# A fused two-attention kernel: maxima 56 units ahead instead of 64, shifts in a group's fourth step, and another end for the last group

## The reference

```python
xn = _layernorm(x)
# A: 8 heads; queries and keys of 128 + 32 dims, both from latents of 32 dims
c_q, c_kv = xn @ W_DQ + b_DQ, xn @ W_DKV + b_DKV
attn = softmax(einsum(q, k) / sqrt(160));  A = (attn @ v_c) @ W_O + b_O
# B: 16 heads of 16 dims. Each token is 'pos' or not, from its query's cosine
# with a guide vector, scaled by the minimum and maximum over all tokens
x_pos, x_neg = masked_attn(pos), masked_attn(~pos)
tok_out = where(pos, x_pos, x_neg)    # each token sees the keys of its own kind
reg_out = (x_pos[:, :5] + x_neg[:, :5]) * 0.5     # the first five tokens
B = concat([reg_out, tok_out]) @ W_proj + b_proj
out = x + A + B
```

## Time and profile before

| | |
|---|---|
| median of three runs | 2928.48 us (2927.09 to 2930.65) |
| the profiled execution | 2925.61 us |
| its span, first to last instruction | 2923.8 us |
| PE busy | 2791.4 us, 95% |
| DVE busy | 2260.7 us, 77% |
| ACT busy | 1649.1 us, 56% |
| POOL busy | 1376.4 us, 47% |
| mean granted TensorE clock | 0.985 |
| chain that ended last | PE 66%, DVE 12%, POOL 12%, issue 4%, DMA 3% |
| PE waits with an empty pipeline | 28.6 us for POOL in the first pass, 15.2 us for shifts, 13.4 us for POOL at the end |

### The profile page before, as it was taken

One profiled execution on the slowest core, in us unless ns is written; L12 is line 12 of the kernel. 1 busy time (PEld: TensorE's weight loads), 2 busy tenths in 40 slices (PEclk: granted clock), 3 DMA queues, 4 the chain that ended last, 5 costly groups with the idle time before them and its releaser, 6 DMA issues.

```text
span 2923.8 us, 45386 instructions
## 1 busy us (share of the span) xinstructions
PE 2791.4 (95%) x16873; PEld 1255.4 (43%) x16873; DVE 2260.7 (77%) x4151; ACT 1649.1 (56%) x1899; POOL 1376.4 (47%) x643
## 2 busy tenths in 40 slices
PE   6888999999999999999999999999999999999997
PEld 4643434443345343453334433453434533344333
DVE  5776887777877888778877788778887788777891
ACT  2444566555655556555665557555665556655674
POOL 6657422692228712395225922278122962259201
PEclk9999999999999999999999999999999999999998
DMA  5524234401352124511344013530244112540001
GB/s 173 188 44 91 70 96 100 87 17 46 101 108 59 33 60 107 114 27 36 88 106 87 18 37 105 103 68 21 64 116 105 36 36 80 115 87 17 22 14 38
DMA packets 129149, 213.45 MB, mean 73 GB/s; under 512 B 47889, under 2 KB 76561, under 8 KB 128753
## 3 DMA queue, kind: packets, MB, share of 16 engines
q1 hardware_dynamic: 125120, 203.21, 29.2%
q10 hardware_dynamic: 3808, 7.34, 0.7%
HBM read 138.31 MB, written 72.50 MB: 72 GB/s over the span
## 4 chain that ended last, share of the span: by engine, by line
PE 66%; DVE 12%; POOL 12%; issue 4%; DMA 3%; ACT 2%; SPq 1%; POOLq 0%; ACTq 0%; DVEq 0%
PE O L1252 20%; PE M L1139 12%; DVE mx L1472 9%; PE M L1133 8%; POOL PTx L848 7%; PE S L1240 6%; PE S L1237 6%; PE M L1167 4%; POOL PT L848 3%; PE M L1217 2%; PE M L1219 2%; PE M L1179 1%; PE M L1185 1%; ACT PT L1002 1%; PE M L1163 1%
## 5 line engine op out<-in xcount | busy, mean ns | idle before, releaser
L1472 DVE TENSOR_REDUCE mx<-M 128x1 f32<-128x512 f32 x3072 | 1949.8, 682 | 374.3 <-PE M L1133 186.0
L1002 ACT ACTIVATE PT<-S 128x1024 f32<-128x1024 f32 x1280 | 1240.1, 1022 | 757.5 <-PE S L1240 480.5
L1139 PE MATMUL M<-KB,QB 50*128 50x512 f32 x2048 | 619.7, 477 | 29.8 <-DVE mx L1472 12.4
L1252 PE MATMUL O<-PT,VB 128*32 128x512 f32 x4096 | 552.3, 611 | 2.3 <-ACT PT L1002 2.3
L1139 PEld LDWEIGHTS M<-KB,QB 50*128 50x128 f32 x2048 | 253.6, 184 | 641.9 <-DVE mx L1472 330.9
L1133 PE MATMUL M<-KA,QA 98*128 98x512 f32 x1024 | 418.6, 458 | 8.0 <-DVE mx L1472 6.5
L1240 PE MATMUL S<-QB,KB 52*128 52x512 f32 x2048 | 377.7, 432 | 8.8 <-ACT PT L1002 7.8
L1002 ACT ACTIVATE PTx<-S 128x1024 f32<-128x1024 f32 x256 | 248.3, 1022 | 194.3 <-PE S L1237 160.7
L1237 PE MATMUL S<-QA,KA 114*128 114x512 f32 x1024 | 318.3, 412 | 15.2 <-DMA QA<-sh_d 15.2
L848 POOL TENSOR_TENSOR PT<-PT,PTx 128x2048 f32<-128x2048 f32 x64 | 293.0, 4578 | 21.3 <-POOL PT L848 10.4
L848 POOL TENSOR_TENSOR PTx<-PTx,PT 128x2048 f32<-128x2048 f32 x64 | 292.1, 4569 | 15.8 <-POOL PTx L848 13.8
(11 more groups left out here) (155 smaller groups left out, 2074.6 us busy)
## 6 DMA issues: line engine op xcount, KB each, us to landing
qk_d<-stg SPq DMA_DIRECT2D x32, 1024.0 KB
KA<-kt_d SPq DMA_DIRECT2D x48, 512.0 KB, 7.3
QB<-qk_d SPq DMA_DIRECT2D x192, 128.0 KB
KB<-qk_d SPq DMA_DIRECT2D x192, 128.0 KB
kt_d<-stg SPq DMA_DIRECT2D x16, 1024.0 KB
RB<-recb_d SPq DMA_DIRECT2D x64, 256.0 KB
PT<-in_x SPq DMA_DIRECT2D x8, 1024.0 KB, 7.1
RB<-rec_d SPq DMA_DIRECT2D x32, 256.0 KB
```

What stands on the lines that cost most here:

```text
L1002: nc.scalar.activation(probs(kind, of_a)[:, 2 * pair:2 * pair + 2, :], Sg[pair][:, :].rearrange("p (j s) -> p j s", j=2), ACT.Exp, scale=S ...
L1139: done = mm(m[:, :], QB[rows, 2 * q + a, at:at + P], KB[rows, 2 * q + a, keys], start=True, stop=True)
L1252: last = mm(O[32 * jj:32 * jj + 32, :], lhs, probs(kind, k)[:, jj, :], start=(c == 0), stop=(c == NC - 1), skip_group_check=True)
L1472: v.tensor_reduce(mx[:, g % 2, unit, kh:kh + 1], m[:, :], AX.X, ALU.max).then_inc(free, 1)
```

## The change

- `prep_jobs`: the 32 first units stand at 13 places, three and two in turn, and the first shift stands two places before the end of the first pass instead of at its end.
- `place` takes the units from one stream over all groups, `LEAD` = 56 units ahead of their step instead of 64. The four steps of batch 0's A that held six units hold four (`FIRST_MAXIMA`); the last batch has units in its steps 48 and 49 of B, which had none.
- `TURN` = 3: every shift stands in the fourth step of a group, not the second. In the first A the last one stands at step 27 instead of 25.
- The last `dn` of a batch stands in B's fifth step instead of the third.
- SP loads the residual of the second half right after it has stored the first half, in B's last group and ahead of `recs` of group 6. POOL adds the constant to it at the end of B, ahead of `clear_z`. `scale` of group 6 comes ahead of the first quad's additions.
- In the first A, the wait for the transfers of constant rows into KB stands ahead of the last shift and not ahead of the first `load_b`.
- The last group of the last batch is finished in another way: PE computes the output blocks from the other groups into the score banks, DVE takes numerators and denominators of the last group from PSUM, 128 queries at a time, inverts and multiplies, PE adds the last product and DVE adds the residual; SP stores block by block. In every batch DVE's inverse of B's group 6 stands after step 60 of B instead of after step 63.

```diff
-    for i in range(16):
-        out[15 + i] += ma[2 * i:2 * i + 2]
-    out[31] += [("fa", "a", 0)]
+    for i in range(13):
+        out[15 + i] += ma[(5 * i + 1) // 2:(5 * i + 6) // 2]
+    out[29] += [("fa", "a", 0)]
...
+LEAD, TURN = 56, 3
...
-FIRST_MAXIMA = (7,) * 4 + (5,) * 12 + (4,) * 2 + (6, 4, 4, 6, 4, 4, 6, 4, 4, 4, 6, 4, 4, 4)
+FIRST_MAXIMA = (7,) * 4 + (5,) * 12 + (4,) * 2 + (4,) * 14
...
-            s[g * NC + 1][2].append(("fa", "b", g + 1))
+            s[g * NC + TURN][2].append(("fa", "b", g + 1))
...
-    s[2][2].insert(0, ("dn", QUADS - 1))
+    for k in range(STEPS_B):
+        place(s[k], "b", LEAD + 4 * (STEPS_A + k), more)
+    s[4][2].insert(0, ("dn", QUADS - 1))
...
 # SP, a_steps
-                if before and g == 0:
-                    load_residual(b, 1)
...
 # SP, b_steps
                 if g == 7:
                     store_out(b, 0, [b_spot(b, last, ("po", c)) for c in range(4)])
-                    if last:
-                        load_residual(b, 1)
+                    load_residual(b, 1)
                 if g:
                     recs(b, "b", g - 1)
...
 # POOL
             if before:
                 clear_z(n)
+            if before:
+                scale(b, "b", GB - 2)
             for i in range(QUADS):
                 add(n, i)
-                if before and i == 0:
-                    residual(b, 1)
-                if before and i < 2:
-                    scale(b, "b", GB - 2 + i)
+                if before and i == 1:
+                    scale(b, "b", GB - 1)
...
 # POOL, end of b_steps
+            residual(b, 1)
...
 # PE
+        def tail():
+            pe.wait_ge(o_done, B * GROUPS - 2)
+            for c in range(4, NC):
+                at = c * P
+                for q in range(QA_):
+                    mm(tail_bank(c), OA[:, q, at:at + P], NA[:, q, :], start=(q == 0), stop=False)
+                mm(tail_bank(c), OB[:, 0, at:at + P], Wp[:, 0, :], start=False, stop=False)
+            pe.wait_ge(o_done, B * GROUPS - 1)
+            for c in range(4, NC):
+                mm(tail_bank(c), OB[:, 1, c * P:(c + 1) * P], Wp[:, 1, :], start=False, stop=False)
+            for c in range(4, NC):
+                pe.wait_ge(tail_ready, c - 3)
+                mm(tail_bank(c), tail_val[:, (c - 4) * P:(c - 3) * P], Wp[:, 1, :], start=False, stop=True
+                   ).then_inc(tail_full, 1)
...
 # DVE
+            for i in range(4):
+                own.link(v.stream_shuffle(tail_rec[:, cols], O[:, cols], [a % DB for a in range(32)]))
+                own.link(v.reciprocal(tail_rec[:, cols], tail_rec[:, cols]))
+                v.scalar_tensor_tensor(tail_val[:, cols], O[:, cols], upper[:, 1:2], tail_rec[:, cols], ALU.mult, ALU.mult
+                                       ).then_inc(tail_ready, 1)
+                if i:
+                    leave(i - 1)
+            leave(3)
```

More of the change, by code:

```diff
@@ L72, in prep_jobs, with place @@
     out[11] = fill_jobs("kt1")
[L73 to L95 removed]
+    for i in range(13):
+        out[15 + i] += ma[(5 * i + 1) // 2:(5 * i + 6) // 2]
+    out[29] += [("fa", "a", 0)]
+    return out
+LEAD, TURN = 56, 3
+STREAM = [u for g in range(GA) for u in max_units("a", g)] + [u for g in range(GB) for u in max_units("b", g)]
+def place(step, kind, at, more):
+    if at >= len(STREAM) and not more:
+        return
+    units = [STREAM[(at + i) % len(STREAM)] for i in range(4)]
+    if kind == "a" and units[0][0] == "ma":
+        step[0] += units[0:1]
+        step[2] = units[2:3] + step[1] + step[2] + units[3:]
+        step[1] = units[1:2]
+    else:
+        step[1] += units[0:2]
+        step[2] = units[2:4] + step[2]
+FIRST_MAXIMA = (7,) * 4 + (5,) * 12 + (4,) * 2 + (4,) * 14
 def place_first(s):
[L100 removed]
+    units = iter(STREAM[32:])
     for step, n in zip(s, FIRST_MAXIMA):
@@ L146, in jobs_a @@
     for g in range(GA):
-        at = (5, 12, 18, 25)[g] if first else g * NC + 1
+        at = (5, 12, 18, 27)[g] if first else g * NC + TURN
         s[at][1].append(("fa", "a", g + 1) if g + 1 < GA else ("fa", "b", 0))
@@ L161, in jobs_a @@
         place_first(s)
[L162 to L166, removed]
+    for k in (() if first else range(STEPS_A)):
+        place(s[k], "a", LEAD + 4 * k, True)
     for i in range(QUADS - 1):
@@ L702, in a_steps @@
                     leave_extremes()
+                if not before and g == GA - 1:
+                    wait_apart(sp, ones_in, 32)
                 shift(n, kind, nxt, a_spot(n, b, ("fa", kind, nxt)))
@@ L773, in _ @@
         b_steps(B - 1, True)
-        dens(B - 1, "b", GB - 1)
-        recs(B - 1, "b", GB - 1)
-        store_out(B - 1, 1, [tail_spot(("po", c)) for c in range(4, NC)])
-        wait_apart(sp, out_done, PRIMED + B * 32)
+        for i in range(4):
+            wait_apart(sp, tail_out, i + 1)
+            at = HALF + i * P
+            sp.dma_start(out[B - 1, at:at + P, :], XR[:, i, :]).then_inc(out_done, 16)
+        wait_apart(sp, out_done, PRIMED + B * 32 + 3 * 16)
     @block.gpsimd
@@ L916, in _ @@
         b_steps(B - 1, True)
-        residual(B - 1, 1)
         scale(B - 1, "b", GB - 2)
-        scale(B - 1, "b", GB - 1)
     @block.scalar
@@ L1328, in _ @@
         values(B - 1, STEPS_B - 1, "b")
-        for j in TAIL:
-            job(j, tail_spot(j), B - 1, B - 1, True)
+        tail()
     @block.vector
@@ L1627, in _ @@
         b_steps(B - 1, True)
-        invert(B - 1, "b", GB - 1)
-        for j in TAIL:
-            job(j, tail_spot(j), B - 1, B - 1)
+        tail()
 def kernel(**inputs):
```

36 lines of the change are left out of this document (23 added, 13 removed).

## The result

The changed kernel took 2970.63 us (median of 4 runs, 2968.25 to 2975.27), the kernel before 2929.47 us beside it. The ratio is 1.0146 [1.0134, 1.0158]: 1.5% slower. The forecast was 2961, its own range 2937 to 2986. The profiled execution has a span of 2966.2 us against 2923.8, so 42.4 us are to be explained.

What follows compares the result with a forecast made beforehand. The prediction took POOL to bound the A stages. Borders +58, front -10.2, tail -11.3, last B's extra units +1.4 and shared steps -5 gave +33, so a median of 2961 us, range 2937 to 2986.

Steps and rivals of the forecast that it cites:

- What bounds an A stage: A stages: POOL, busy 118.11 of 123 us and never without work, is the bound and hands its lateness on.
- Rival A: A stages: they do not follow POOL, so its late start is absorbed; -33 us, 2895, chance 12%.
- The border: Seven borders between a B and the next A: POOL's additions start 13.0 us later; 8.3 us each, 58 us together.
- a backlog that moves as a whole: Border, SP: the 17.7 us from first load to landing of the `qk3` store move along with the later shift.
- Rival B: Border: the store of `qk3` lands where it did despite later loads; 1.6 us a border, 2914 in all, chance 14%.
- Rival C, the clock: PE's stop in each A: its clock falls to the 1.2 GHz level; 21 us more, 2982, chance 14%.
- The front: First pass and batch 0: earlier first shift 5.5, moved wait for constants 2.5, fewer units a step 2.2; 10.2 us gained.
- the 5.5 us for the earlier first shift: Front: transposing the first shift before the last two query sets gains 5.5 us, between 2 and 7.06.
- the cost of the later `dn` in B's fifth step: B's early steps: the shift behind `dn` on SP comes 5.4 us later; cost 0, at worst 1 us a batch.
- moving the wait for the constants: Front, the 8.16 us wait: the move removes a bubble, not the transfers; 2.5 us gained, between 0 and 8.16.
- The end: Tail behind the last values: the new finish of the last group gains 11.3 us, between 9 and 14.5.
- Shared steps: B's steps holding a shift and half a fill: 5 us gained, with 12 us to either side.

Runs made afterwards that it cites:

- e1: Changed kernel with the residual loaded at the start of A again, and POOL's constant and group 6's `scale` back among the additions; 2937.0 us.
- e2: Changed kernel with SP's loads for heads 2 moved behind the store of `qk3`, `store_out`, the residual's load and `recs` of group 6; 2959.0 us.
- e4: Changed kernel with the first pass as before: two units at each of 16 places and the first shift at the last; 2969.5 us.
- e6: e2 plus `recs` of group 7 ahead of `load_z`, group 6's `recs` and `scale` ahead of the residual, batch 0's `load_z` ahead of `dens` and shift; 2900.6 us.
- e8: e1 with `recs` of group 7 ahead of `load_z` on SP; 2915.8 us.
- e12: e10 plus `recs` of group 6 ahead of the store of `qk3`, and the first pass's units and first shift as in the kernel before; 2874.5 us.
- e3: Kernel before with the new end alone, and the inverse of B's group 6 after step 60; 2914.1 us.
- e7: Kernel before's shifts, lead, `dn` and front, with the new end and the residual out of the A stage on e6's orders; 2912.5 us.
- e9: e6 with output blocks, `store_out` and the residual earlier in B, and loads for heads 2 and 3 behind group 7's `dens` and `recs`; 2901.4 us.
- e10: e9 with the fill ahead of the shift in the five steps of a B that hold both; 2880.0 us.

## Why the prediction was right, point by point

- **What bounds an A stage: right, and shown.** In the table, start plus length less A's four groups is 6.5 to 6.6 us in e1, e2, e4 to e6 and e8 to e12 and in the changed kernel, and 7.3 to 7.4 in before, e3 and e7, with A stages from 118.3 to 128.0 us. Within its work there POOL has no gap over 0.6 us in the changed kernel, and in the others none over 1.3 us except the wait for the broadcast at `scale` of group 7. Rival A (2895) is out.
- **The border: right in mechanism, 0.9 us a border too dear.** 8.3 us were said; it is (62.8 - 10.8) / 7 = 7.4. The start moved 11.7 us (13.0 said) and the length fell by 3.5 (3.6 said), which is 8.2. A's four groups grew by 9.0, as the additions now end 6.5 us behind the last take-out instead of 7.3, and 1.5 came back in B's first group (1.14 said). e1 and e8 show that the residual's order is the cause: undone, A's first group is 28.3 us.
- **The step "a backlog that moves as a whole": right for this order.** First load to landing was 17.7 us and is 16.1. The store alone lands 4.15 us behind its issue (1895.93 to 1900.08 in e9), 5.0 in e2 and 8.5 behind the loads. Rival B (2914) is out as the order stood. The Trainium skill (DMA: Bandwidth & Descriptors, Anatomy of one DMA) spoke for that rival with an estimated 4.4 us for this store, from a cost that it gives for transfers issued by GpSimd; SyncE issues this one. With nothing ahead of it in e9 the trace agrees with the estimate (4.15 us); behind the loads it does not (8.5 us), and the measurement decides.
- **Rival C, the clock: it fell, and cost next to nothing.** Granted clock 0.51 behind the stop, but POOL paced the stage: the offset of 6.6 us is the same with a stop (changed) and without (e6).
- **The front, -10.2: wrong.** Measured +4.6 up to the end of B's group 2. The step that failed first is the 5.5 us for the earlier first shift, with its bounds. Its transpose, two places earlier in the order, came at 152.10 us, 1.5 later than before, and the first scores at 156.67, where 152 was said. PE no longer waits for the shift (0.60 us, was 7.06) but for DVE: 4.23 us at the next units, and up to 3.6 us (2.45 before) at a place with three units. e4 and e12 show no gain, if anything 1 to 4 us lost, and the first take-out is at 204.8 to 207.8 us in the five profiles with the old first pass and at 205.5 to 211.2 in the nine with the new one. The second failed step is the cost of the later `dn` in B's fifth step, "0, at worst 1 us a batch": the row sums in batch 0 waited 5.3 us for Z, and e6 got them back. Only the shift behind it on SP was priced, and not `load_z` behind both. What moving the wait for the constants gave stays open: the wait of 8.16 us was 4.66, but it was 3.84 in e3, whose code is the old one there. Nor is the size of +4.6 sure: e3 and e7, with the old code up to that place, are 2.6 and 7.8 us later there than the kernel before. A gain of 10.2 us shows in no profile.
- **The end, -11.3: right**, 12.7 in the trace, 13.3 in e3. The products took 7.2 us (6.9 said), DVE's part behind them 5.2 (5.2 said); landing took 2.1 us instead of 3.6.
- **Shared steps, -5: wrong in sign**, +8.0. The order within the step decides: shift first +8.0, fill first -12.6 (137.0 to 135.2, seven times; e10). The sum took the term from an argument and not from a row, with 12 us to either side (-17 to +7); the order that was built came out just above that, and the other one inside it. The sign "B's groups as long as before within 0.5 us" did not hold either.
- **What the sum did not have**: the 10.2 us less in B's groups 1 and 2, for the most part because the granted clock falls less often than before.

Against the sum of +33 the trace has +42.4. The front was put 14.8 us too low and the shared steps 13.0; the borders were put 6.0 too high, the end 1.4, the last B 0.7, and B's groups 1 and 2 gave 10.2 that no term had. So the total owes something to errors that cancel; its main term does not.

## What to carry to other kernels

When one engine is without a gap through a stage, the stage's end follows its start plus its length (here at a constant distance, 6.5 or 7.3 us), so write down both for every variant: here an edit that shortened one often lengthened the other. Where a late chain is repaired, look for a second one behind it on the same queue, because the first hides it; here moving one `recs` ahead of one `load_z` was worth 39 us in one kernel and 21 in another. And within a step, put the work that needs nothing (the fill) ahead of what two engines pass to and fro (the shift).

## What the runs showed of the hardware

- A small store behind 1.5 MB of loads: 4 x 512 values took 8.3 us from issue to landing (901.76 to 910.07, e2), and 1.75 (1905.57 to 1907.32) where such loads stood behind it on SP (e9).
- The granted clock of B's groups 1 and 2 is 0.88 to 0.95 in some batches of the kernel before and 1.00 in others with the same instructions. Shifts, lead and `dn` of the change, together, make such falls rarer (the sums above are some 12 us less over seven batches); what sets them off stays open.
- The first pass differs by up to 6 us between executions of the same code (first take-out of A at 205.5 in e10, 211.2 in e9), so that a single profile says little of the front.
